# Softmax denominator of an attention stage: from one TensorE matmul per key group to an fp32 running sum on VectorE

## The reference

```python
q = rms_norm(x @ Wq.T)   # 16 heads of 128
k = rms_norm(x @ Wk.T)   # 4 kv heads of 128, each used by 4 query heads
v = x @ Wv.T
attn = softmax(q @ k.T * 128 ** -0.5)
y = attn @ v
vn = v / norm(v)
y = y - sum(y * vn, axis=-1) * vn
return y @ Wo.T
```

## Time and profile before

| | us |
|---|---|
| median of the three timed runs | 4979.28 |
| the three runs | 4711.35, 4979.28, 5056.25 |
| the profiled execution, its own time | 4709.49 |
| its span on the slowest core (core 4) | 4707.9 |
| spans of the eight cores | 4684.6 to 4707.9 |
| TensorE busy in the span | 3395.5 (72%) |
| VectorE busy in the span | 1599.7 (34%) |
| ScalarE (ACT) busy in the span | 1424.0 (30%) |

### The profile page before, as it was taken

One profiled execution on the slowest core, in us unless ns is written; L12 is line 12 of the kernel. 1 busy time (PEld: TensorE's weight loads), 2 busy tenths in 40 slices (PEclk: granted clock), 3 DMA queues, 4 the chain that ended last, 5 costly groups with the idle time before them and its releaser, 6 DMA issues.

```text
span 4707.9 us, 49763 instructions; the slowest of 8 cores (4684.6 to 4707.9 us)
## 1 busy us (share of the span) xinstructions
PE 3395.5 (72%) x14582; PEld 1309.7 (28%) x14582; DVE 1599.7 (34%) x3212; ACT 1424.0 (30%) x1714; POOL 96.0 (2%) x155
## 2 busy tenths in 40 slices
PE   1445577877888888888888885354268888888991
PEld 0222233333222222222222221122123333333440
DVE  0333577776343443343344333123210000000004
ACT  0111233333666555666655664011000000000001
POOL 0000000000000000000000000000000000000010
PEclk9767799999888888898888887666689999999995
DMA  8000322221000000000000002411322222233444
GB/s 143 18 18 27 135 98 96 93 99 50 3 3 3 3 3 3 3 3 3 3 3 5 3 1 72 97 59 49 37 52 54 56 54 54 54 56 56 69 72 146
DMA packets 74706, 218.87 MB, mean 46 GB/s; under 512 B 16232, under 2 KB 42344, under 8 KB 61120
## 3 DMA queue, kind: packets, MB, share of 16 engines
q0 software_dynamic: 55632, 91.95, 12.1%
q1 hardware_dynamic: 18816, 123.74, 7.6%
HBM read 279.26 MB, written 28.31 MB: 65 GB/s over the span
## 4 chain that ended last, share of the span: by engine, by line
PE 66%; DVE 19%; issue 4%; ACT 4%; DMA 3%; another core or an unknown queue 3%; DVEq 1%; POOL 0%; ACTq 0%; SPq 0%; POOLq 0%
PE S_ps L167 11%; PE yT_ps L167 9%; PE gps L167 7%; PE dn_ps L167 7%; PE ups L167 7%; PE ops L167 6%; PE kps L167 5%; PE vps L167 4%; PE wops L167 3%; PE qps L167 3%; DVE rdn_sb L167 2%; DVE st L167 2%; DVE xnT L167 2%; DVE khat L167 1%
## 5 line engine op out<-in xcount | busy, mean ns | idle before, releaser
L167 ACT ACTIVATE P_sb<-S_ps 128x1024 bf16<-128x1024 f32 x1024 | 1048.7, 1024 | 697.7 <-PE S_ps L167 464.9
L167 DVE TENSOR_TENSOR padd<-P_sb 128x512 bf16<-128x512 bf16 x1024 | 435.2, 425 | 897.6 <-PE yT_ps L167 334.2
L167 PE MATMUL S_ps<-qth,KT_sb 128*128 128x512 bf16 x2048 | 678.3, 419 | 17.3 <-ACT P_sb L167 13.7
L167 PE MATMUL yT_ps<-P_sb,V_sb 128*128 128x512 bf16 x2048 | 645.0, 398 | 4.7 <-ACT P_sb L167 4.7
L167 PE MATMUL dn_ps<-padd,onec_sb 128*1 128x512 bf16 x1024 | 400.5, 391 | 64.3 <-DVE padd L167 64.2
L167 PE MATMUL kps<-wk_sb,xnT 128*128 128x512 bf16 x1024 | 406.1, 397 | 0.4
L167 PE MATMUL vps<-wv_sb,xnT 128*128 128x512 bf16 x1024 | 405.2, 396 | 0.0
L167 PE MATMUL gps<-xn2T,wg_sb 128*128 128x512 bf16 x1376 | 318.0, 385 | 15.6 <-DMA wu_sb<-wu_r 15.4
L167 DVE TENSOR_TENSOR hid<-sg_sb,ups 128x512 bf16<-128x512 bf16 x86 | 59.2, 689 | 781.0 <-ACT sg_sb L167 781.0
L167 PE MATMUL ops<-wdq_sb,hid 128*128 128x512 bf16 x1376 | 310.0, 386 | 17.8 <-DMA wdq_sb<-wd 10.0
L167 PE MATMUL ups<-xn2T,wu_sb 128*128 128x512 bf16 x1376 | 311.0, 379 | 0.0
(11 more groups left out here) (145 smaller groups left out, 2178.4 us busy)
## 6 DMA issues: line engine op xcount, KB each, us to landing
xa<-x_my SPq DMA_DIRECT2D x72, 1024.0 KB, 4.8
wg_sb<-wg_r POOLq DMA_DIRECT2D x43, 512.0 KB, 6.3
wu_sb<-wu_r POOLq DMA_DIRECT2D x43, 512.0 KB, 8.2
wdq_sb<-wd POOLq DMA_DIRECT2D x40, 512.0 KB, 5.3
wq_sb<-wqT POOLq DMA_DIRECT2D x1, 8192.0 KB, 77.9
wo_sb<-woT POOLq DMA_DIRECT2D x4, 2048.0 KB, 42.9
out<-x_sb SPq DMA_DIRECT2D x8, 1024.0 KB, 5.6
x2r_sb<-out SPq DMA_DIRECT2D x8, 1024.0 KB, 6.8
```

The costliest lines, as they stand in the source:

```text
L167: instr = getattr(eng, op)(*a, **kw)
```

## The change

The denominator's matmul of each group is gone. VectorE keeps two running sums `pacc0` and `pacc1` (128x512 in fp32) of `padd`, for even and for odd groups; groups 0 and 1 start them with a copy. At the end of a block two fp32 matmuls with a fp32 column of ones, `onecf_sb`, bring the two sums to `dn_ps`. The value `paddd[g]`, for which the exp of group g+4 waits, now counts the add to the running sum too.

The division moves behind the correction. VectorE copies `yT_ps` to `yTs_sb` without it. Four fp32 matmuls with one column each turn the reciprocals into a column per piece, `rdnT_ps`, which VectorE copies to `rdnT_sb`; the correction's fused operation writes to `cscr`, and a further instruction multiplies that by the column into `Y_sb`. Each of the five instructions of a piece now has a wait for VectorE's own last instruction ahead of it. `bc_ps`, `bc_sb`, the copy and the multiplication with them are gone. One small load, `onecf_sb`, is added at the start of the program.

```diff
+        gq.dma(g.dma_start(out=onecf_sb[:, :], in_=onecf))
...
-                        pe.wait(v, dnd.get(g - 2, 0))
                         dve.inc(v.tensor_tensor(padd[g % 2][:, :], P_sb[g % 4][:, 0:512],
                                                 P_sb[g % 4][:, 512:1024], ALU.add))
+                        dve.wait(v)
+                        if g < 2:
+                            pe.wait(v, dn_mm)
+                            dve.inc(v.tensor_copy(pacc[g % 2][:, :], padd[g % 2][:, :]))
+                        else:
+                            dve.inc(v.tensor_tensor(pacc[g % 2][:, :], pacc[g % 2][:, :],
+                                                    padd[g % 2][:, :], ALU.add))
                     paddd[g] = dve.n
...
-                        dve.wait(te, paddd[g])
-                        pe.inc(te.matmul(
-                            dn_ps[:, :], onec_sb[:, :], padd[g % 2][:, :],
-                            start=(g == 0), stop=(g == NG - 1)))
                     pv_done[g] = pe.n
...
+                dve.wait(te, paddd[NG - 1])
+                pe.inc(te.matmul(dn_ps[:, :], onecf_sb[:, :], pacc[0][:, :], start=True, stop=False))
+                pe.inc(te.matmul(dn_ps[:, :], onecf_sb[:, :], pacc[1][:, :], start=False, stop=True))
...
                 dve.inc(v.reciprocal(rdn_sb[:, :], dn_ps[:, :]))
+                dve.wait(v)
+                dve.inc(v.tensor_copy(yTs_sb[:, :], yT_ps[:, :]))
...
-                pe.inc(te.matmul(bc_ps[:, :], onerf_sb[:, :], rdn_sb[:, :], start=True, stop=True))
...
-                dve.inc(v.tensor_copy(bc_sb[:, :], bc_ps[:, :]))
-                dve.wait(v)
-                dve.inc(v.tensor_tensor(yTs_sb[:, :], yT_ps[:, :], bc_sb[:, :], ALU.mult))
...
+                for j in range(4):
+                    pe.inc(te.matmul(rdnT_ps[:, j:j + 1], rdn_sb[0:1, j * 128:(j + 1) * 128],
+                                     onerf_sb[0:1, 0:1], start=True, stop=True))
...
+                dve.inc(v.tensor_copy(rdnT_sb[:, :], rdnT_ps[:, :]))
...
-                    dve.inc(v.scalar_tensor_tensor(
+                    dve.inc(v.scalar_tensor_tensor(cscr[:, :], vnv, dot_sb[:, 1:2], yv,
+                                                   ALU.mult, ALU.add))
+                    dve.wait(v)
+                    dve.inc(v.tensor_scalar(
                         Y_sb[:, qt * D + h * 128: qt * D + (h + 1) * 128],
-                        vnv, dot_sb[:, 1:2], yv, ALU.mult, ALU.add))
+                        cscr[:, :], rdnT_sb[:, j:j + 1], None, ALU.mult))
```

More of the change, by code:

```diff
@@ L107, in build @@
     onec = nc.dram_tensor("onec", [128, 1], BF16, kind="ExternalInput").ap()
+    onecf = nc.dram_tensor("onecf", [128, 1], F32, kind="ExternalInput").ap()
     onerf = nc.dram_tensor("onerf", [1, 128], F32, kind="ExternalInput").ap()
@@ L127, in build @@
     onec_sb = ctx.enter_context(nc.sbuf_tensor("onec_sb", [128, 1], BF16))
+    onecf_sb = ctx.enter_context(nc.sbuf_tensor("onecf_sb", [128, 1], F32))
     onerf_sb = ctx.enter_context(nc.sbuf_tensor("onerf_sb", [1, 128], F32))
@@ L698, in build @@
     padd = [bC.enter_context(nc.sbuf_tensor(f"padd{i}", [128, 512], BF16)) for i in range(2)]
+    pacc = [bC.enter_context(nc.sbuf_tensor(f"pacc{i}", [128, 512], F32)) for i in range(2)]
+    rdnT_sb = bC.enter_context(nc.sbuf_tensor("rdnT_sb", [128, 4], F32))
     qth = [bC.enter_context(nc.sbuf_tensor(f"qth{i}", [128, TPC], BF16)) for i in range(2)]
@@ L701, in build @@
     rdn_sb = bC.enter_context(nc.sbuf_tensor("rdn_sb", [1, 512], F32))
-    bc_sb = bC.enter_context(nc.sbuf_tensor("bc_sb", [128, 512], F32))
     yTs_sb = bC.enter_context(nc.sbuf_tensor("yTs_sb", [128, 512], BF16))
@@ L709, in build @@
     dn_ps = bC.enter_context(nc.psum_tensor("dn_ps", [1, 512], F32))
-    bc_ps = bC.enter_context(nc.psum_tensor("bc_ps", [128, 512], F32))
+    rdnT_ps = bC.enter_context(nc.psum_tensor("rdnT_ps", [128, 4], F32))
     tt_ps = bC.enter_context(nc.psum_tensor("tt_ps", [128, 512], BF16))
@@ L716, in build @@
     qth_loaded = [0, 0]
+    dn_mm = 0
     epi_done = dve.n
@@ L806, in _ @@
                                 start=(g == 0 and j == 0), stop=(g == NG - 1 and j == 1)))
-                        dve.wait(te, paddd[g])
-                        pe.inc(te.matmul(
-                            dn_ps[:, :], onec_sb[:, :], padd[g % 2][:, :],
-                            start=(g == 0), stop=(g == NG - 1)))
                     pv_done[g] = pe.n
-                    dnd[g] = pe.n
+            @on("tensor")
+            def _(te):
+                dve.wait(te, paddd[NG - 1])
+                pe.inc(te.matmul(dn_ps[:, :], onecf_sb[:, :], pacc[0][:, :], start=True, stop=False))
+                pe.inc(te.matmul(dn_ps[:, :], onecf_sb[:, :], pacc[1][:, :], start=False, stop=True))
+            dn_mm = pe.n
             @on("vector")
@@ L816, in _ @@
                 dve.wait(v)
+                pe.wait(v, dn_mm)
                 pe.wait(v, pv_done[NG - 1])
                 dve.inc(v.reciprocal(rdn_sb[:, :], dn_ps[:, :]))
+                dve.wait(v)
+                dve.inc(v.tensor_copy(yTs_sb[:, :], yT_ps[:, :]))
             rdn_done = dve.n
+            ydiv_done = dve.n
+            epi_done = dve.n
             @on("tensor")
@@ L823, in _ @@
                 dve.wait(te, rdn_done)
-                pe.inc(te.matmul(bc_ps[:, :], onerf_sb[:, :], rdn_sb[:, :], start=True, stop=True))
-            bcast_done = pe.n
-            @on("vector")
-            def _(v):
-                dve.wait(v)
-                pe.wait(v, bcast_done)
-                dve.inc(v.tensor_copy(bc_sb[:, :], bc_ps[:, :]))
-                dve.wait(v)
-                dve.inc(v.tensor_tensor(yTs_sb[:, :], yT_ps[:, :], bc_sb[:, :], ALU.mult))
-            ydiv_done = dve.n
-            epi_done = dve.n
+                for j in range(4):
+                    pe.inc(te.matmul(rdnT_ps[:, j:j + 1], rdn_sb[0:1, j * 128:(j + 1) * 128],
+                                     onerf_sb[0:1, 0:1], start=True, stop=True))
+            rdnT_done = pe.n
             @on("tensor")
@@ L848, in _ @@
                 dve.wait(v)
+                pe.wait(v, rdnT_done)
+                dve.inc(v.tensor_copy(rdnT_sb[:, :], rdnT_ps[:, :]))
                 pe.wait(v, ytr_done)
@@ L1582, in prep_inputs @@
         ebias=ebias, eye=np.eye(128, dtype=BF), eyef8=np.eye(8, dtype=np.float32),
-        onec=np.ones((128, 1), BF),
+        onec=np.ones((128, 1), BF), onecf=np.ones((128, 1), np.float32),
         onerf=np.ones((1, 128), np.float32), consts=consts,
```

## The result

The changed kernel is slower: its time is 1.0504 times that of the kernel before (95% interval 1.0473 to 1.0534). It takes 4941 to 4979 us (median 4947), the kernel before 4711 to 4719. The span of core 1 grew from 4700.1 to 4927.9 us.

A forecast was written before the change was run, and what follows sets the result against it. It took ACT and TensorE to bound the loop equally at 1.28 us per group, then VectorE at 1.385. 31 blocks x 7.0 = 217 us, plus 5.7, 1.0 and 0.5, gave +224 on 4709.5: 4935 us, range 4850 to 5060.

The forecast's parts named there:

- VectorE's group 1.385 us: Loop, groups 2 to 31: padd 0.425, fp32 add 0.69, waits 0.10 and 0.17, making VectorE the new bound.
- ACT's floor of 1.28: Loop: ACT's work and four waits take 1.28 us per group, so a shorter TensorE period buys nothing at high clock.
- The copies in groups 0 and 1: Loop start: copying bf16 padd to the fp32 sums takes 0.48 us each, 1.25 us per group with waits.
- The fp32 sums at the low clock: Block end: two fp32 sum matmuls take 4.1 us after TensorE idles, 4.4 with semaphore and waits.
- `rdnT` and the transposes: Epilogue: semaphore 0.15, four small fp32 matmuls 1.4, then transposes to the correction's first multiply 0.7; together 2.2 us.
- The correction 6.9 us: Epilogue: four pieces of 1.73 us each, with a new column multiplication of 0.22 and five waits; before, 4.95 + 0.1.
- The first block +5.7: First block, without a correction ahead: from VectorE's start to its reciprocal, ending at 1210.1 instead of 1204.4 us.
- The stages outside attention, +0.5: Before attention: the additional load delays the first stage by one DMA start, 0.5 us.
- the add at the rate of bf16: Rival, loop: VectorE's group takes 1.12 us, ACT's 1.28 binds again, 4697 us, no change; 4%.
- The low clock in the loop: Rival, loop: pauses drop TensorE's clock to 1.2 GHz, four matmuls take 1.71 us per group, 5053 us; 7%.
- The high clock for the sums: Rival, block end: sum matmuls meet a high clock, 1.9 us less per block, 4874 us; within the forecast's 0.87.
- The gain that TensorE's share seems to promise: Rival, block starts: if VectorE's waits cost nothing, low-clock groups shorten, 77 us in all, 4633 us; 1 to 2%.

## Where the prediction failed, what held, and which terms were off

**The step that failed is the base of the sum.** The prediction added its 224 us to one execution, 4709.5 us, and gave the result as an absolute time, 4935, in a range of 4850 to 5060. The metric's own figure for the kernel before was the median of the three timed runs, 4979.3 us, and these ran from 4711 to 5056. Against that median, 4935 says 0.9% shorter, the opposite of what the sum says. The runs showed 1.0504 times the time of before, which on the median's base is 5230 us and outside the range. The prediction saw the 5.7% between its two bases and answered it with one sentence; what its working supports is a ratio, 1.048, and not a time.

**Some terms were mis-sized too.** On its own base the forecast was 4.8% longer, and measured is 5.04%, that is 4947 us. The block came out at 62.3 us instead of 61.7, that is 7.65 instead of 7.0 more, and 237 us instead of 217. The mechanism held at every step that a run touched. The sizes, step by step (core 1, means over the blocks where nothing else is said):

- *VectorE's group 1.385 us, binding through `paddd`.* Measured 1.395; the add 693 ns (taken: 690), the gaps 0.10 and 0.17. Right, and shown to be the cause by the runs without the add and with it in bf16.
- *ACT's floor of 1.28, TensorE's relief worth nothing in mid-block.* Right: exps stay at 1.28 us without the matmuls.
- *The copies in groups 0 and 1, 0.48.* They take 0.427, as long as a bf16 add. All 32 groups together are 44.1 us in the block shown, as forecast, and 44.4 in the mean.
- *The fp32 sums at the low clock, 4.4 us with their waits (4.1 for the matmuls, bounds 2.2 and 4.1).* VectorE's idle time ahead of the 32 reciprocals is 123.7 us, 3.87 each: -0.5 us per block. The low clock came as forecast, but the price was wrong at both bounds. The prediction took twice the recorded 1.09 or 2.04 us of the old fp32 matmul. The four instructions here start 0.85 us apart at the clock 0.50, and only the last one counts with its recorded 1.06, together 3.57; at 1.00 they start 0.43 apart, together 1.88. The sentence ahead of the rows, that the distance of the starts tells more than the duration, applies to this term. The reading that the clock is 0.50 behind a pause of 3.60 us was weak as well: in the earlier trace rows the matmul behind that pause takes 1.09, and 22 of the 32 such matmuls of the kernel before (core 4) take less than the 2.04 us of the low clock. Why the pause ahead of the sums finds the clock low more often is not shown.
- *`rdnT` and the transposes 2.2 us.* From the cast's end (1829.25) to the correction 2.7 us: eight small fp32 instructions take 1.84 us, 0.23 each, not 0.17. +0.5 per block.
- *The correction 6.9 us.* 7.2 in the block shown (1831.95 to 1839.18, with the two waits ahead of `padd`), 7.3 in the mean: the new operation takes 0.255 instead of 0.22, and the waits a little more than 0.10 each. +0.4 per block.
- *The first block +5.7*: 1151.0 to 1201.5 against 1158.3 to 1203.8, +5.0. *Behind the last reciprocal +1.0*: 14.2 us against 12.3 until `Y_sb` is stored, +1.9.
- *The stages outside attention, +0.5.* They were 16 us shorter on this core than before. No term foresaw it and no run explains it; the first reciprocals of the eight cores of the kernel before already lie 9 us apart (1196.3 to 1205.5). That the span grew by 228 us, close to the 224 of the sum, is in part luck: these 16 us stand against the 20 us that the blocks took more.

The rivals: the add at the rate of bf16 did not occur by itself but only when the type was changed. The low clock in the loop did not occur: 1.00 over 37.3 us of a block's middle, with TensorE 67% busy and 0.37 us of pause in each group. The high clock for the sums did not occur by itself either; it took the filled pause. The Trainium skill (TensorE: Matmul & The Clock Gate, "A second HAM failure mode: psum-queue depth-cycling") would have short pauses between groups of matmuls make the clock go back and forth; this trace does not agree for pauses of 0.37 us. The gain that TensorE's share seems to promise was refuted by the run without the denominator's matmuls, which gave 2.3% while nothing was put in their place; the add that was put there costs, with its wait, 5.4% (268 of 4947 us).

## What to carry to other kernels

Before moving work from a busy engine to an idle one, work out the period of each engine per iteration, its waits included: here an engine that was 40% busy had 0.86 us to spare in 1.28, and 0.69 of work with 0.27 of gaps between the operations went beyond that by 0.11 us in nearly each of 1024 groups. Where two engines have the same period, relieving one shows nothing; look at the second engine's list of waits first, above all at waits for its own last instruction. Keep all operands of an elementwise add at 16 bits where the precision allows it, and let the accumulation in fp32 happen in PSUM.

## What the runs showed of the hardware that I had not expected

- A wait of ACT for its own last instruction cost at least 0.27 us per exp (1.225 us from exp to exp with three waits, this one among them; 0.954 with the other two), five times the 0.055 us of another wait. Without it the exps start 0.954 us apart although each is recorded with 1.024.
- The releaser in a row can name an engine whose relief changes nothing: 0.26 us "<-PE" before, "<-ACT" when TensorE had less to do, with not a hundredth of difference in the gap.
- Fp32 matmuls of 512 columns that stand back to back cost less than their recorded durations: four instructions recorded with about 1.06 us each at the granted clock 0.50 took 3.57 together, and four of 0.59 at 1.00 took 1.88.
- 16 matmuls for nothing, put into a pause of 3.7 us, shortened the fp32 matmuls behind them from 3.4 to 1.9 us and the kernel by 1%.
